# A second-layer FFN block split over other steps, and other step tables for the last two tiles, in a fused macaron layer

## The reference

```python
def ffn(x):                      # k0, k1, k2 are boolean: weights of +1 and -1
    h = concatenate([x, -x], axis=-1)
    h = relu(s0 * (h @ w(k0))) * 2       # 256 -> 512
    h = relu(s1 * (h @ w(k1))) * 2       # 512 -> 512
    return s2 * (h @ w(k2))              # 512 -> 128

def attn(x):                     # 16 heads of 8 features, 256 tokens a sequence
    Q, K, V = x @ Wq.T + bq, x @ Wk.T + bk, x @ Wv.T + bv    # by heads
    p = softmax(Q @ K.T / sqrt(8))
    return layernorm(p @ V + x, gamma, beta)

x = x + 0.5 * ffn(layernorm(x))
x = x + attn(layernorm(x))
x = x + 0.5 * ffn(layernorm(x))
```

## Time and profile before

| | |
|---|---|
| median of 3 runs | 748.02 us (747.82 to 748.07) |
| the profiled execution's own time | 748.17 us |
| its span, first to last instruction | 746.3 us |
| mean granted clock of TensorE | 0.995 |
| PE busy | 700.1 us, 94% |
| DVE busy | 649.3 us, 87% |
| ACT busy | 510.5 us, 68% |
| POOL busy | 365.3 us, 49% |

### The profile page before, as it was taken

One profiled execution on the slowest core, in us unless ns is written; L12 is line 12 of the kernel. 1 busy time (PEld: TensorE's weight loads), 2 busy tenths in 40 slices (PEclk: granted clock), 3 DMA queues, 4 the chain that ended last, 5 costly groups with the idle time before them and its releaser, 6 DMA issues.

```text
span 746.3 us, 18730 instructions
## 1 busy us (share of the span) xinstructions
PE 700.1 (94%) x7363; PEld 338.0 (45%) x7363; DVE 649.3 (87%) x1270; ACT 510.5 (68%) x745; POOL 365.3 (49%) x650
## 2 busy tenths in 40 slices
PE   7779999999999999999999999999999999787887
PEld 3434343444444454444444444444445444343436
DVE  6677898989999899999989898999989998878866
ACT  3426767777677777777787777767777776666744
POOL 6531455564454547454463746445454743253430
PEclk9998999999999999999999999999999999999999
DMA  3101010201102020100102020110201010010000
GB/s 81 51 21 48 20 52 3 65 17 45 37 3 66 17 65 17 62 20 27 41 16 66 16 66 17 44 38 2 67 17 65 17 42 27 30 38 2 11 7 29
DMA packets 29526, 25.65 MB, mean 34 GB/s; under 512 B 4352, under 2 KB 29440, under 8 KB 29440
## 3 DMA queue, kind: packets, MB, share of 16 engines
q1 hardware_dynamic: 27824, 23.74, 9.9%
q10 hardware_dynamic: 1616, 0.72, 0.3%
HBM read 5.05 MB, written 4.19 MB: 12 GB/s over the span
## 4 chain that ended last, share of the span: by engine, by line
PE 71%; DVE 18%; ACT 3%; issue 3%; POOL 3%; SPq 1%; DMA 0%; DVEq 0%; POOLq 0%
PE ps_c L879 15%; PE ps_z L704 13%; PE ps_z L705 11%; PE ps_s L826 9%; DVE row_max L1513 8%; DVE ffn_lo L1388 5%; PE ps_z L694 3%; PE ps_z L695 3%; PE ps_z L686 2%; PE ps_m L811 2%; PE ps_m L800 2%; PE ps_c L800 2%; ACT ffn_hi L1123 2%; PE ps_z L715 1%; PE ps_m L785 1%
## 5 line engine op out<-in xcount | busy, mean ns | idle before, releaser
L1513 DVE TENSOR_REDUCE row_max<-ps_s 128x4 f32<-128x1024 f32 x256 | 312.1, 1219 | 34.4 <-PE ps_s L826 32.7
L1162 ACT ACTIVATE probs<-ps_t,score_scale 128x1024 f32<-128x1024 f32 x252 | 280.2, 1112 | 63.6 <-PE ps_t L839 61.2
L1123 ACT ACTIVATE ffn_hi<-ps_z 128x512 f16<-128x512 f32 x261 | 149.7, 595 | 80.4 <-PE ps_z L705 65.4
L704 PE MATMUL ps_z<-ffn_hi,w 128*128 128x512 f16 x464 | 177.9, 383 | 0.9
L705 PE MATMUL ps_z<-ffn_lo,w 128*128 128x512 f16 x464 | 176.6, 381 | 0.0
L1388 DVE SCALAR_TENSOR_TENSOR ffn_lo<-ps_z,ffn_hi 128x512 f16<-128x512 f32 x232 | 154.1, 683 | 18.0 <-ACT ffn_hi L1123 14.9
L879 PE MATMUL ps_c<-probs,v_cols 128*32 128x256 f32 x2048 | 131.0, 384 | 1.3 <-ACT probs L1162 0.7
L826 PE MATMUL ps_s<-k_rows,q_rows 32*128 32x256 f16 x1024 | 100.4, 273 | 12.5 <-DVE row_max L1513 10.8
L839 PE MATMUL ps_t<-q_rows,k_rows 32*128 32x256 f16 x992 | 96.9, 273 | 0.0
L879 PEld LDWEIGHTS ps_c<-probs,v_cols 128*32 128x32 f32 x2048 | 56.8, 109 | 53.5 <-issue 25.7
L826 PEld LDWEIGHTS ps_s<-k_rows,q_rows 32*128 32x128 f16 x1024 | 29.0, 92 | 101.2 <-issue 51.1
(11 more groups left out here) (225 smaller groups left out, 1106.4 us busy)
## 6 DMA issues: line engine op xcount, KB each, us to landing
x<-L_attn_x SPq DMA_DIRECT2D x16, 256.0 KB, 2.7
q_rows<-q_hi SPq DMA_DIRECT2D x32, 128.0 KB, 2.5
k_rows<-k_hi SPq DMA_DIRECT2D x31, 128.0 KB, 2.1
y<-x SPq DMA_DIRECT2D x15, 256.0 KB, 2.2
q_rows<-no_max SPq DMA_DIRECT2D x16, 128.0 KB, 2.1
q_rows<-q_lo SPq DMA_DIRECT2D x16, 128.0 KB, 2.1
k_rows<-k_lo SPq DMA_DIRECT2D x15, 128.0 KB, 2.1
q_rows<-max_rows SPq DMA_DIRECT2D x64, 8.0 KB
```

The source lines that it names most:

```text
L704: pe.matmul(o[:], w, ffn_hi[:, 1 + k, :], start=(k == 0), stop=False)
L1123: a_.activation(ffn_hi[:, use, :], ps_z[use % 2][:], ACT.Relu if use else ACT.Copy, scale=1.0 if use else XN_SCALE).then_inc(z_hi, 1)
L1162: a_.activation(probs[n % PROBS][:, j:j + 2, :], o[:], ACT.Exp, scale=score_scale[:, 0:1]).then_inc(s_exp, 1)
L1513: v.tensor_reduce(row_max[hb % 2][:].rearrange("p (a l) e -> p l a e", a=2)[:, j:j + 2, :, g % 2], ps_s[:].rearrange("p l (a k) -> p l a k ...
```

## The change

`FFN_MID` moves one pair of the fourth block from piece 12 to 11 and one from 13 to 12, so that piece 13 holds one pair. `maxima_first` no longer holds for piece 13: in the step behind it DVE takes the fourth block's low part ahead of the row maximum. In iterations 14 and 15 the FFN's pieces lie on steps 4 to 31 (before 9 to 31, and 7 to 31), their input's statistics and norm come earlier, the steps of the projections are other ones, K goes through ps_c as elsewhere, the warm products are left out, and POOL's `att_norm` for the last tile stands at the end of iteration 13, where the tail statistics come in step 25. `tail_base` stands earlier in POOL's queue of these two iterations. In iteration 0 the transposes and Q come in steps 15 and 17. `project` leaves out one wait for K.

```diff
@@ -43,14 +43,13 @@
 PACE_ZERO = {6 + piece * 21 // 15: piece for piece in range(PIECES)}
-PACE_ALONE = {9 + piece * 22 // 15: piece for piece in range(PIECES)}
-PACE_LAST = {7 + piece * 24 // 15: piece for piece in range(PIECES)}
+PACE_ALONE = {4 + piece * 27 // 15: piece for piece in range(PIECES)}
...
 AT = {"LNT": 6, "Q": 8, "K": 11, "CT0": 14, "CT1": 22, "V": 25}
-AT_ALONE = {"LNT": 6, "CT0": 9, "Q": 11, "K": 14, "CT1": 22, "V": 28}
-AT_ZERO = {"LNT": 13, "Q": 16, "K": 20, "V": 23}
+AT_ALONE = {"LNT": 5, "Q": 8, "K": 11, "CT0": 14, "CT1": 22, "V": 28}
+AT_ZERO = {"LNT": 15, "Q": 17, "K": 20, "V": 23}
 AT_OWN_LAST = {"CT0": 7, "CT1": 19}
@@ -67,21 +66,21 @@
 WARM_ONE = {22: 3, 26: 4, 28: 4, 30: 4}
-WARM_ALONE, WARM_LAST = {6: 4, 8: 7}, {6: 5}
 AT_STATS_A, AT_STATS_B, AT_STATS_PREP = ((2, 2, 9, 9), 10), ((24, 24, 25, 25), 27), ((18, 18, 20, 20), 26)
-AT_STATS_A_ALONE = ((2,) * TT, 3)
+AT_STATS_A_ALONE = ((0,) * TT, 1)
 AT_STATS_B_ZERO, AT_STATS_PREP_ZERO = ((20, 20, 23, 23), 24), ((28, 28, 30, 30), 31)
 AT_STATS_NEXT_ZERO = ((7,) * TT, 8)
-AT_NORM_A_ALONE = (7, 5)
+AT_NORM_A_ALONE = 3
 AT_STATS_B_ONE = ((8, 8, 10, 10), 11)
...
 AT_STATS_SOLO = (27, 28)
-AT_STATS_TAIL, AT_STATS_TAIL_ALONE, AT_STATS_TAIL_EARLY = (16, 30), (16, 28), (11, 22)
+AT_STATS_TAIL, AT_STATS_TAIL_ALONE, AT_STATS_TAIL_EARLY = (16, 30), (18, 26), (11, 22)
+AT_STATS_TAIL_BEFORE = (16, 25)
...
 FFN_IN = {2: 0, 3: 1, 4: 2, 5: 3}
-FFN_MID = tuple((6 + n, 2 * n, 2 * n + 2) for n in range(8))
+FFN_MID = ((6, 0, 2), (7, 2, 4), (8, 4, 6), (9, 6, 8), (10, 8, 10), (11, 10, 13), (12, 13, 15), (13, 15, 16))
 FFN_MID_DONE = {7: 0, 9: 1, 11: 2, 13: 3}
@@ -108,6 +107,7 @@
         self.first = t == 0 or t == 1
+        self.last_full = prep and prev and pace is None and next_b is None
         self.at = AT_OWN_LAST if own_contexts else AT_ZERO if not prev else AT_ALONE if pace else AT
@@ -302,7 +302,7 @@
                 Iteration(T - 1, 1, prep=False, ffn_a=second_ffn(T - 3), misc_base=6 * (T - 1) + 2,
-                          pace=PACE_LAST, own_contexts=True)]
+                          pace=PACE_ALONE, own_contexts=True)]
         L, L_PAR, L_USE = T - 1, (T - 1) % 2, 6 * (T - 1) + 4
@@ -332,17 +332,13 @@
-        def k_apart(it):
-
-            return it.at is not AT_ALONE
-
         def at_max_last(it):
...
-            return (AT_STATS_TAIL_EARLY if it.own_contexts else AT_STATS_TAIL_ALONE if it.pace and it.prev
+            return (AT_STATS_TAIL_EARLY if it.own_contexts else AT_STATS_TAIL_BEFORE if it.last_full else AT_STATS_TAIL_ALONE if it.pace and it.prev
                     else AT_STATS_TAIL)
@@ -625,13 +621,15 @@
                 alone = it.pace and it.stats_a
-                if it.prep and it.prev:
+                if it.prep and it.prev and not alone:
                     att_norm(t + 1, 1 - par)
...
                 split_max(t, 0)
+                if alone:
+                    tail_base(t, par)
                 if not it.prev:
@@ -648,8 +646,6 @@
                     split_max(t, 2)
-                if alone:
-                    tail_base(t, par)
                 if it.prev:
@@ -660,6 +656,8 @@
                     tail_norm(t - 1, 1, 1 - par)
+                if it.last_full:
+                    att_norm(t + 2, par)
                 if it.own_contexts:
@@ -790,7 +788,6 @@
                 else:
-                    at_least(pe, m_free, use)
                     at_least(pe, c_free, pairs_done[0])
@@ -977,9 +974,6 @@
                         warm(WARM_ONE[s], ps_z[0][:])
-                    elif it.pace and it.prev and s in (WARM_LAST if it.own_contexts else WARM_ALONE):
-                        pe.wait_ge(z_free, Z_USES * it.ffn_a - 1)
-                        warm((WARM_LAST if it.own_contexts else WARM_ALONE)[s], ps_z[0][:])
                     pieces = [(f, piece) for f, _, piece in ffn_work(it, s)]
@@ -987,7 +981,7 @@
                         context(tile, parity, g,
-                                k_use=it.misc["K"] if it.prev and it.prep and k_apart(it) and s == HALF else None)
+                                k_use=it.misc["K"] if it.prev and it.prep and s == HALF else None)
                     if it.prev and s == at_max_last(it):
...
@@ -1598,7 +1592,7 @@
                     pieces = ffn_work(it, s - 1)
-                    maxima_first = any(piece in FFN_MID_DONE for _, _, piece in pieces)
+                    maxima_first = any(piece in FFN_MID_DONE and piece != FFN_MID[-1][0] for _, _, piece in pieces)
                     if maxima_first and it.cur and s % 2 == 0:
@@ -1639,8 +1633,8 @@
                         if s - 1 == at(it, "K"):
-                            qk_rest(t + 1, 1, ps_c if k_apart(it) else ps_m)
-                    if it.pace and it.stats_a and s == AT_NORM_A_ALONE[it.own_contexts]:
+                            qk_rest(t + 1, 1, ps_c)
+                    if it.pace and it.stats_a and s == AT_NORM_A_ALONE:
                         ffn_apply(it.ffn_a, x2[par])
```

More of the change, by code:

```diff
@@ L998, in steps @@
                                 context_transpose(t - 1, b, it.misc[f"CT{b}"],
-                                                  behind_k=b == 0 and it.prep and k_apart(it))
+                                                  behind_k=b == 0 and it.prep)
                     if it.prep:
@@ L1011, in steps @@
                         if s == at(it, "K"):
-                            project(1, it.misc["K"], ps_c if k_apart(it) else ps_m)
+                            project(1, it.misc["K"], ps_c)
             run(pe, steps)
@@ L1239, in steps @@
                         if s == at(it, "K"):
-                            qk_split(1, it.misc["K"], ps_c if k_apart(it) else ps_m)
+                            qk_split(1, it.misc["K"], ps_c)
             run(act, steps)
```

## The result

The changed kernel takes 763.80 us as a median of 4 runs (762.97 to 764.90), against 748.05 for the kernel before beside it: a ratio of 1.0208, with a 95% interval from 1.0196 to 1.0220. The forecast was 763. The profiled execution took 762.97, with a span of 761.2.

The account below looks back on a forecast made before the run. PE was taken to bound the kernel, but only just (busy 41.91 of 42.7 us, DVE 39.23). The terms 15.4 + 4.8 - 0.1 - 3.0 - 1.0 - 1.0 = +15.1 on 748.17 gave 763, range 757 to 769.

Parts of the forecast that it names:

- The new wait in step 11: PE at the fourth block's first pair, ahead of K, waits 0.80 for block 2's low part to free its bank.
- The first half: Later row maximum 6 delays the next FFN's low part and PE's step 18 product: +1.23 per iteration, 12.5 times, +15.4.
- Where the removed wait went: Third layer's 0.38 wait goes, but scores of step 16 wait for row maximum 7, starting at 436.99 against 436.31.
- The second half: Later tail statistics delay POOL's att_xn and PE's step 6 transposes: +0.44 per iteration, 11 times, +4.8.
- Iteration 1: Has other statistics between, so counted as half a full iteration's first-half cost, between 0 and 1.23.
- Iteration 13: Pays the first half's 1.23 and the second half's 0.44, with -0.1 for the hand-over to iteration 14.
- Iteration 14: FFN starting at step 4 instead of 9 and 11 warm products dropped: -3.0, with the gain between 0 and 8.1.
- Iteration 15: New tables with contexts and transposes kept in place: -1.0, between 0 and -6.4, near nothing as most order stays.
- The head: Iteration 0: transposes moved to step 15 remove PE's 1.20 wait for att_xn in step 13: -1.0, between 0 and -4.
- That PE alone bounds: Rival: the pair does not wait in step 11 and DVE has slack before step 18, giving 731; chance 0.08.
- That DVE catches up: Rival: DVE catches up before step 18 and POOL before step 6; only 0.68 per iteration remains, 752; chance 0.10.
- The clock: Rival: new waits in steps 11 and 18 drop the clock to 1.2 GHz in every iteration, giving 797; chance 0.03.

Follow-up runs that it names:

- e2: The kernel before with the split alone changed (pair 12 in piece 11, pairs 13 and 14 in piece 12): 765.72 us, ratio 1.0234.
- e4: The changed kernel with DVE also taking the second block's low part ahead of its row maximum (piece 9): 752.84 us, ratio 1.0059.
- e1: The kernel before with the order alone changed (fourth block's low part ahead of the row maximum behind piece 13): 750.57 us, ratio 1.0028.
- e5: The changed kernel with the second tail statistics of every full iteration in step 25 instead of 30: 760.22 us, ratio 1.0160.
- e3: The changed kernel with the split and order of before, so only the tables of iteration 0 and the last two differ: 745.63 us, ratio 0.9967.
- e7: e6 with the new order of e1 added, pairs still two to a piece: 742.89 us, ratio 0.9928.
- e6: e3 with the tail statistics of full iterations in steps 18 and 25 instead of 16 and 30: 748.54 us, ratio 0.9995.
- e10: The changed kernel with iteration 0's step table of before (first transposes at step 13, Q at 16): 764.43 us, ratio 1.0209.
- e11: e8 with the step tables of before in iteration 15 and in iteration 0: 739.45 us, ratio 0.9870.
- e8: e7 with the new order in full iterations alone, iterations 14 and 15 keeping the old order: 741.76 us, ratio 0.9914.

## Why the prediction was right, and where its terms were not

The bound, the place of the new wait, its size and what it pushes were as forecast; the time, 763 against 763.8, is better than its terms, since some errors cancel.

- **The new wait in step 11**: 0.80 forecast, 0.79 measured, ahead of the K projection, behind block 2's low part, which kept its place behind row maximum 5. DVE's idle time ahead of row maximum 6 was forecast as 1.6 and is 1.60. **The first half**: +1.23 forecast, +1.17 measured. e2 and e4 show that the split is the cause and the bank the wait.
- **Where the removed wait went**: the third layer no longer waits for the fourth block in the first half, as forecast (0.5 is left, in the second half), and the scores of step 16 come late for row maximum 7. e1 shows it without the split: from 1.2 to 0.2, and still not faster.
- **The second half**: +0.44 forecast, 0.29 measured, with a wait of 0.35 at the transposes; e5 got back 0.36 by moving the tail statistics alone. The mechanism was right and the term too large by 0.15. The tail statistics themselves come as late as forecast: 42.89 behind the iteration's first row maximum (467.42) instead of 41.26, 0.46 more than the first half's 1.17. Most of the 0.15 is got back behind the transposes of step 6, where the next product starts 0.46 after them (431.85 to 432.31) and before the change 0.60 (422.37 to 422.97).
- **Iteration 1**, taken as half a full iteration, +0.6, was +0.50. Iteration 13, where the statistics come in step 25, was +0.93, where the terms give 1.23 + 0.44 - 0.1. All full iterations and iteration 1: +17.5 measured, +20.1 forecast.
- **Iteration 14**: -3.0 forecast, -2.15 measured, in the range of 0 to -8.1. The tables alone give -2.74 (e3); the split and the order, for which the forecast has no term here, take 0.59 back.
- **Iteration 15**: -1.0 forecast, and +0.49 measured, +0.96 with what lies behind it. This term had the wrong sign. The forecast gave no mechanism for it ("near nothing as most of its order stays"); the step that failed is the gain it gave the new tables there, and that it put the split and the order at nothing. The tables alone, in e3, take 36.99, 0.17 more than before, and 0.11 less behind it: they are worth nothing. They bring new waits, those of DVE for ACT (1.1 in the kernel before) and of PE for the norm at the FFN's first transposes (not listed there). In iteration 15 of the changed kernel:

```profile
DVE ffn_lo L1382 <- ACT ffn_hi L1117: 3.3, 3, 1.7
...
PE ps_z L684 <- DVE ffn_xn L1421: 1.1, 1, 1.1
```

  And of e3, the same:

```profile
DVE ffn_lo L1382 <- ACT ffn_hi L1117: 3.3, 3, 1.7
...
PE ps_z L684 <- DVE ffn_xn L1421: 1.1, 1, 1.1
```

  So these waits are not what the changed kernel loses against e3. Up to row maximum 11 the two run alike to 0.01. Row maximum 12 then comes 0.44 later, waiting for scores, which in the changed kernel have the moved pair ahead of them:

```profile
712.00 1.23 DVE L1507 TENSOR_REDUCE row_max<-ps_s 128x4 f32<-128x1024 f32 x1 [0.54 <-PE ps_s L823]
```

  0.32 of that is left at the last row maximum (37.31 against 36.99). Behind it lie 41.04 against 40.46, a cost that comes with the order: without the split it is 41.19 in e7 against 40.72 in e6.

- **The head**: -1.0 forecast, -1.40 measured (-0.94 ahead of iteration 0 and -0.46 in it), and for other reasons. The forecast put the gain into iteration 0's step table; at the same clock that table loses 2.2 (e10, e11 and the lengths above). The gain came from the wait on m_free that `project` leaves out, which the forecast had at nothing, looking at iteration 15 alone. It also stands ahead of iteration 0. The timeline of PE in the kernel before, at the projections of the first tile (Q in ps_m, K in ps_c) and its first scores:

```profile
30.62 0.39 PE L800 MATMUL ps_m<-att_hi,wt_hi 128*128 128x512 f16 x1 [0.79 <-DVE att_lo L1499]
...
33.22 0.39 PE L800 MATMUL ps_c<-att_hi,wt_hi 128*128 128x512 f16 x1 [1.14 <-DVE q_lo L1504]
...
39.41 0.39 PE L826 MATMUL ps_s<-k_rows,q_rows 32*128 32x256 f16 x4
```

  And in the changed kernel:

```profile
30.99 0.39 PE L797 MATMUL ps_m<-att_hi,wt_hi 128*128 128x512 f16 x1 [0.79 <-DVE att_lo L1493]
...
32.29 0.38 PE L797 MATMUL ps_c<-att_hi,wt_hi 128*128 128x512 f16 x1
...
38.48 0.39 PE L823 MATMUL ps_s<-k_rows,q_rows 32*128 32x256 f16 x4
```

  From Q to K it was 2.60 and is 1.30, and from Q to the first scores 8.79 and 7.49: the whole 1.30 reaches the scores. The runs agree: iteration 0 starts at 40.76 to 41.43 in the three profiled kernels with this wait (before, e1, e2) and at 39.54 to 40.04 in the eleven without it, e10 among them, which has the old table. The row at 33.22 stands in the trace of before, but the forecast read only iterations and not what stands ahead of them. The rest is small: Q itself starts 0.37 later in this execution, and iteration 0 is 0.46 shorter, by a table that loses and a clock that did not fall.

- **The rivals.** That PE alone bounds (731) fell with the wait in step 11. That DVE catches up (752) fell with the low part at 449.21, which is as late as row maximum 6 makes it. The clock did not go down in the full iterations: 1.00 in the window of iteration 9, with a wait of 0.79 in it. What the prediction draws on, a kernel that cycled through PSUM banks, stands in the Trainium skill, TensorE: Matmul & The Clock Gate, in the section "A second HAM failure mode: psum-queue depth-cycling". The trace does not agree with it here, since this bank wait of 0.79 stands in every full iteration at 1.00. The Trainium skill, TensorE: Matmul & The Clock Gate, section "HAM oscillation — how this bites in real kernels", tells of groups of matmuls with DMA waits between them that are longer than the groups, and a clock that drops after each of them. The waits of the full iterations are far shorter than the work between them (0.79 in 44.2 us), and no run of this case shows waits of that kind; what the runs show is that the full iterations of no kernel profiled here lost the clock, with waits of PE up to that 0.79, and that the first and the last iterations of some did.

## What to carry to other kernels

Where two banks alternate, a product that is moved earlier can meet its bank still held: here (e2) its result came no earlier, PE waited for the bank, and everything that stands behind the product in PE's queue paid for it. Before an operation is put ahead of another on an engine with a gapless run, look up who waits for the one that is put back: here the order took away 1.0 of waits per iteration, and 0.58 of it arrived, and only once the tail statistics were out of the way (e7 against e6). A wait that is left out should be looked up at every place where its code runs, the start of the program too.

## What the runs showed of the hardware that was not expected

The clock fell in some executions and not in others, after the same work. e8 and e3 run the same program in iteration 0, and up to row maximum 6 DVE's instructions there start at the same distance from the first row maximum to 0.01 us. The timelines of PE in iteration 0, two lines with idle time ahead of them, of e8 (1.00 in all of iteration 0):

```profile
50.90 0.39 PE L823 MATMUL ps_s<-k_rows,q_rows 32*128 32x256 f16 x4 [1.06 <-DVE row_max L1507]
...
55.22 0.39 PE L823 MATMUL ps_s<-k_rows,q_rows 32*128 32x256 f16 x4 [1.13 <-DVE row_max L1507]
```

And of e3, with a granted clock of one half, 1.2 GHz, from 54.8 to 58.2:

```profile
50.74 0.39 PE L823 MATMUL ps_s<-k_rows,q_rows 32*128 32x256 f16 x4 [1.06 <-DVE row_max L1507]
...
55.06 0.60 PE L823 MATMUL ps_s<-k_rows,q_rows 32*128 32x256 f16 x4 [1.13 <-DVE row_max L1507]
```

The idle times are the same (1.06, then 1.13), and the last line shows scores that take 0.60 instead of 0.39. What decides between the two is not shown. One such fall costs 1.5: iteration 0 takes 39.70 in e3 and 38.22 in e8. Runs of the changed kernel differ by that: 762.97 and 763.09 at a mean granted clock of 1.000, 764.50 and 764.90 at 0.997 and 0.995. So in the first and last iterations of this kernel a difference of 2 us between two profiles says nothing until their granted clocks have been compared.
